# A two-layer graph network on one core: rings of eight for the last layer's rows, loaded by GpSimd, and bias rows as three bf16 parts

## The reference, cut to what matters

```python
# layer 0: messages over all edges, a sum for each destination, an MLP, two norms
m     = silu(concat(x[src], x[dst], edge_attr) @ mW1 + mb1) @ mW2 + mb2
agg   = segment_sum(m, dst, 6250)
h_new = silu(concat(x, agg) @ uW1 + ub1) @ uW2 + ub2
x1    = layernorm(x + layernorm(x + h_new) * gamma + beta)
# layer 1: the mean of the neighbours' new rows, an MLP with relu, a norm
agg   = segment_sum(x1[src], dst, 6250) / maximum(degree, 1)
h     = relu(relu(concat(x1, agg) @ W1 + b1) @ W2 + b2)
out   = layernorm(x1 + h)
```

## Time and profile before

| | |
|---|---|
| median of three runs | 2214.85 us |
| span of the profiled execution | 2215.4 us |
| TensorE busy | 1979.7 us (89%), granted clock 0.936 on average |
| VectorE busy | 1662.3 us (75%) |
| ScalarE busy | 1432.8 us (65%) |
| POOL busy | 1515.0 us (68%), with 455.7 us of "issue" between its gathers |
| DMA | 487.82 MB, mean 220 GB/s |

### The profile page before, as it was taken

How to read it: one execution, slowest core, us unless ns; L and a number is a source line. 1 busy time by engine, 2 the same in 40 slices (tenths; PEclk the granted TensorE clock), 3 DMA queues, 4 the chain that set the end, 5 groups by cost and what they waited for, 6 DMA issues and landing times.

```text
span 2215.4 us, 59812 instructions
## 1 busy us (share of the span) xinstructions
PE 1979.7 (89%) x19664; PEld 1740.5 (79%) x19664; DVE 1662.3 (75%) x5615; ACT 1432.8 (65%) x3734; POOL 1515.0 (68%) x1605
## 2 busy tenths in 40 slices
PE   7888888889988998999998999999989999999774
PEld 7877777777887887887886898987987998988542
DVE  7688877877886877887887788888887788774332
ACT  3677766776776766776776777766766766673122
POOL 7577777777777777777777777777777777770110
PEclk9999989997998997998999999999998999999976
DMA  8477767676687777777877787877877887986822
GB/s 288 139 206 219 201 189 213 175 220 202 187 231 211 210 218 210 216 239 231 241 232 210 241 249 243 269 238 219 254 244 227 272 266 238 293 264 207 268 65 62
DMA packets 307523, 487.82 MB, mean 220 GB/s; under 512 B 120202, under 2 KB 181644, under 8 KB 307208
## 3 DMA queue, kind: packets, MB, share of 16 engines
q10 hardware_dynamic: 102369, 251.46, 34.3%
q1 hardware_dynamic: 154823, 129.94, 19.8%
q0 software_dynamic: 50016, 102.53, 17.9%
HBM read 375.62 MB, written 108.13 MB: 218 GB/s over the span
## 4 chain that ended last, share of the span: by engine, by line
POOL 46%; PE 18%; issue 17%; DMA 8%; DVE 6%; ACT 2%; DVEq 1%; ACTq 0%; SPq 0%; POOLq 0%
POOL gath L858 46%; DMA gath<-P_d,src_i 6%; PE ps_l L1167 4%; PE ps_pre L1114 3%; PE ps_cnt L1131 3%; DVE edgeK L917 2%; PE ps_sum L1151 2%; DMA gath<-x1T_d 1%; DVE pre L930 1%; PE ps_pre L1225 1%; DVE edgeL L915 1%; ACT eT_c L1401 1%; PE ps_pre L1227 1%; PE ps_pre L1117 1%; PE ps_p L432 1%
## 5 line engine op out<-in xcount | busy, mean ns | idle before, releaser
L858 POOL DMA_INDIRECT gath<-P_d,src_i x1535 | 1456.8, 949 | 486.9 <-issue 455.7
L917 DVE TENSOR_SCALAR edgeK<-iotaK,key 128x500 bf16<-128x500 f16 (+1 forms) x1564 | 667.3, 488 | 0.0
L1114 PE MATMUL ps_pre<-wc,eT_c 128*128 128x128 f32 x3128 | 613.7, 318 | 2.4 <-issue 2.4
L1131 PE MATMUL ps_cnt<-edgeK,edgeL 128*128 128x250 bf16 (+1 forms) x3128 | 479.9, 301 | 92.4 <-ACT counts L1269 48.6
L1114 PEld LDWEIGHTS ps_pre<-wc,eT_c 128*128 128x128 f32 x3128 | 508.8, 204 | 25.0 <-issue 2.6
L1269 ACT ACTIVATE counts<-ps_cnt 128x1000 bf16<-128x1000 f32 x391 | 404.4, 1034 | 173.2 <-issue 85.1
L1151 PE MATMUL ps_sum<-edgeN,h 128*128 128x40 f32 x3128 | 421.8, 285 | 55.4 <-ACT h L1325 55.1
L1151 PEld LDWEIGHTS ps_sum<-edgeN,h 128*128 128x128 f32 x3128 | 391.6, 196 | 81.1 <-ACT h L1325 69.1
L930 DVE TENSOR_TENSOR pre<-ps_pre,gath 128x512 f32<-128x512 f32 x384 | 260.9, 680 | 254.9 <-DMA gath<-P_d,src_i 175.7
L1131 PEld LDWEIGHTS ps_cnt<-edgeK,edgeL 128*128 128x128 bf16 x3128 | 288.3, 101 | 162.1 <-DVE edgeK L917 83.4
L1325 ACT ACTIVATE h<-pre 128x512 f32<-128x512 f32 x391 | 243.9, 624 | 262.4 <-DVE pre L930 258.6
(11 more groups left out here) (160 smaller groups left out, 1505.5 us busy)
## 6 DMA issues: line engine op xcount, KB each, us to landing
eT_c<-eT ACTq DMA_DIRECT2D x193, 512.0 KB
A_d<-counts ACTq DMA_DIRECT2D x168, 384.0 KB
rel_c<-rel_d ACTq DMA_DIRECT2D x193, 240.0 KB
A_v<-A_d SPq DMA_DIRECT2D x70, 448.0 KB
A_v<-A_d SPq DMA_DIRECT2D x111, 256.0 KB
gath<-P_d,src_i POOLq DMA_INDIRECT x1535
A_d<-counts ACTq DMA_DIRECT2D x56, 416.0 KB
Qw<-Q_d SPq DMA_DIRECT2D x56, 180.0 KB
```

The lines of the kernel that those rows point to most:

```text
L858: pool.indirect_dma_start(gath[:, q, t * D:(t + 1) * D], None, v["P_d"], bass.IndirectOffsetOnAxis(ap=src_i[g % 2][:, c:c + 1], axis=0)).t ...
L917: last = V.tensor_scalar(edgeK[x][:, ROFF[j]:ROFF[j] + A2 * w], iotaK[j][:, :, 0:A2 * w // KR], key[k][:, q * QT + j:q * QT + j + 1], None ...
L1114: T.matmul(o, eT_c[c % RE][:, e0:e0 + P], wc[:], start=True, stop=False)
L1131: last = T.matmul(o[:, :, w0:w0 + w], edgeL[x][:, j, 0:P], r, start=(j == 0), stop=(j == QT - 1 and q == 0), skip_group_check=True)
```

## The change

Two things change. First, the rings `xT_l` and `x_l` get eight places instead of three (`RL`), in buffers that are free by then: `xT_l` takes all seven parts of `gath` and `xT_u`; `x_l` takes the second halves of the three `eT_c`, the two `h`, and `hT_u`, `z_u`, `xT1_u`. The ring of results `z_l` stays at three (`RZ`). Their loads move from ScalarE's queue to POOL's. The first eight stand ahead of POOL's first mean; the load of unit `w + 6` stands behind the mean of `w`, for `w` of 2 to 6, and waits until TensorE's step 0 and VectorE's step 3 of unit `w - 2` are done. Second, each of the three bias rows is split into three bf16 rows whose sum is the float32 row, in partitions 0, 32 and 64 of a tile of 65 partitions that is otherwise zero. TensorE multiplies 65 rows of ones with it in bf16, in one pass. VectorE makes the parts once, in six instructions for each row, at quads 14 and 21.

```diff
-    xT_l, x_l = [gath[:, i, :] for i in range(3)], [gath[:, 3 + i, :] for i in range(3)]
+    xT_l = [gath[:, i, :] for i in range(GQ)] + [xT_u]
+    x_l = [t[:, UB * D:2 * UB * D] for t in eT_c] + [t[:].rearrange("p t n -> p (t n)") for t in h] + [
+        hT_u, z_u[:].rearrange("p j n -> p (j n)"), xT1_u]
 ...
     def gpsimd(pool):
 ...
+        def load_last(w):
+            cols, n = last_columns(w)
+            r = w % RL
+            if w == 0:
+                pool.wait_ge(pre_add, NQ)
+                pool.wait_ge(sum_mm, NQ)
+            u = next(u for u, (b0, b1, s0) in enumerate(UNITS) if LAST_UNITS[w][1] <= b1)
+            if r >= 5:
+                u = len(UNITS) - 1
+            pool.wait_ge(x1_out, 16 * (u + 1))
+            pool.wait_ge(x1T_out, 16 * (u + 1))
+            if w >= RL:
+                pool.wait_ge(l_hidden, w - RL + 1)
+                pool.wait_ge(l_z, w - RL + 1)
+            pool.dma_start(xT_l[r][:, 0:n * P], v["x1T_d"][:, cols]).then_inc(l_xT_in[r], 16)
+            pool.dma_start(x_l[r].rearrange("p (j n) -> p j n", n=D)[:, 0:n, :],
+                           v["x1_d"][cols, :].rearrange("(j p) n -> p j n", p=P)).then_inc(l_x_in[r], 16)
 ...
+            for w in range(RL):
+                load_last(w)
             for w in range(len(LAST_UNITS)):
 ...
                 nc.gpsimd.tensor_tensor(sumT[:, cols], sumT[:, cols], deg[:, cols], ALU.mult).then_inc(l_mean, 1)
+                if w >= 2 and w + RL - 2 < len(LAST_UNITS):
+                    load_last(w + RL - 2)
 ...
+        def split_bias(k, whole):
+            V.tensor_copy(biases[k][0:1, :], whole[0:1, :])
+            V.tensor_copy(bias_hi[:], whole[:]).then_inc(bias_part, 1)
 ...
+            V.tensor_tensor(bias_rest[:], whole[:], bias_hi[:], ALU.subtract).then_inc(bias_part, 1)
 ...
+            V.tensor_copy(biases[k][32:33, :], bias_rest[32:33, :])
+            V.tensor_copy(bias_mid[:], bias_rest[:]).then_inc(bias_part, 1)
 ...
+            V.tensor_tensor(biases[k][64:65, :], bias_rest[64:65, :], bias_mid[64:65, :], ALU.subtract).then_inc(bias_ready, 1)
 ...
-                T.matmul(ps_y[x][:, 0:n * D], ones_row[:], b2bc[0:1, :].unsqueeze(1).broadcast_to([1, n, D]), start=True, stop=True)
+                T.matmul(ps_y[x][:, 0:n * D], onesb[0:BK, :], biases[2][:].unsqueeze(1).broadcast_to([BK, n, D]), start=True, stop=True)
 ...
-                if w + 3 < len(LAST_UNITS):
-                    load_last(w + 3)
```

More of the change, by code:

```diff
@@ L54 @@
 VB, RA, RT, LEAD, AHEAD = 14, 4, 12, 4, 10
+RL, RZ = 8, 3
 NQ = -(-(-(-N_EDGES // P)) // QT)
@@ L66 @@
 EPS = 1e-5
+BK = 65
 SKIP = 8192
@@ L245, in bass_gnn_two_layers @@
         eps_col = sb("eps_col", [P, 1])
-        ones_row = sb("ones_row", [1, P])
+        biases = [sb(f"bias{k}", [BK, D], BF16) for k in range(3)]
         rdeg_in = sem("rdeg_in")
@@ L396, in gpsimd @@
         pool.memset(onesb[:], 1.0)
-        pool.memset(v["ones_row"][:], 1.0)
+        for b in v["biases"]:
+            pool.memset(b[:], 0.0)
         pool.iota(first_i[:], [[0, 1]], base=0, channel_multiplier=GE * N_NODES // N_EDGES).then_inc(made, 1)
@@ L712, in build_edges @@
     a_in = [sem(f"av_in{r}") for r in range(RT)]
-    l_xT_in, l_x_in, l_out = ([sem(f"l_{n}{i}") for i in range(3)] for n in ("xT_in", "x_in", "out"))
+    l_xT_in, l_x_in = ([sem(f"l_{n}{i}") for i in range(RL)] for n in ("xT_in", "x_in"))
+    l_out = [sem(f"l_out{i}") for i in range(RZ)]
     l_mean, l_hidden, l_relu, l_y, l_z, l_var, l_sd, l_rs, l_norm, l_dv = (
@@ L829, in fast @@
             sp.wait_ge(dg_io, 64 * len(UNITS))
-            for r in range(3):
-                sp.wait_ge(l_out[r], 16 * len(range(r, len(LAST_UNITS), 3)))
+            for r in range(RZ):
+                sp.wait_ge(l_out[r], 16 * len(range(r, len(LAST_UNITS), RZ)))
         def general(sp):
@@ L948, in add_visit, with split_biases @@
                             ALU.add).then_inc(changed, 1)
+        def split_bias(k, whole):
+            V.tensor_copy(biases[k][0:1, :], whole[0:1, :])
+            V.tensor_copy(bias_hi[:], whole[:]).then_inc(bias_part, 1)
+            dve.wait_ge(bias_part, 3 * k + 1)
+            V.tensor_tensor(bias_rest[:], whole[:], bias_hi[:], ALU.subtract).then_inc(bias_part, 1)
+            dve.wait_ge(bias_part, 3 * k + 2)
+            V.tensor_copy(biases[k][32:33, :], bias_rest[32:33, :])
+            V.tensor_copy(bias_mid[:], bias_rest[:]).then_inc(bias_part, 1)
+            dve.wait_ge(bias_part, 3 * k + 3)
+            V.tensor_tensor(biases[k][64:65, :], bias_rest[64:65, :], bias_mid[64:65, :], ALU.subtract).then_inc(bias_ready, 1)
+        def split_biases(s):
+            if s == 2 * GQ:
+                dve.wait_ge(u_in, 160)
+                split_bias(0, ub2bc)
+                split_bias(1, bbc)
+            if s == 3 * GQ:
+                dve.wait_ge(v["l1_in"], 64)
+                split_bias(2, b2bc)
         parts = [0]
@@ L1073, in fast @@
                 unit_step(s)
+                split_biases(s)
                 if g + 1 < GROUPS and q == 2:
@@ L1187, in unit_step @@
                 pe.wait_ge(u_silu, u + 1)
-                T.matmul(ps_u[:, 0:n * D], ones_row[:], ub2bc[0:1, :].unsqueeze(1).broadcast_to([1, n, D]), start=True, stop=True)
+                if u == 0:
+                    pe.wait_ge(bias_ready, 2)
+                T.matmul(ps_u[:, 0:n * D], onesb[0:BK, :], biases[0][:].unsqueeze(1).broadcast_to([BK, n, D]), start=True, stop=True)
                 for j in range(n):
@@ L1197, in unit_step @@
                 pe.wait_ge(u_scaled, u + 1)
-                T.matmul(ps_u[:, 0:n * D], ones_row[:], bbc[0:1, :].unsqueeze(1).broadcast_to([1, n, D]), start=True, stop=True)
+                T.matmul(ps_u[:, 0:n * D], onesb[0:BK, :], biases[1][:].unsqueeze(1).broadcast_to([BK, n, D]), start=True, stop=True)
                 for j in range(n):
@@ L1223, in last_step @@
                     pe.wait_ge(l_relu, w - 1)
-                pe.wait_ge(l_xT_in[w % 3], 16 * (w // 3 + 1))
-                T.matmul(o, w1[:, 0, :], xT_l[w % 3][:, 0:n * P], start=True, stop=False)
+                pe.wait_ge(l_xT_in[w % RL], 16 * (w // RL + 1))
+                T.matmul(o, w1[:, 0, :], xT_l[w % RL][:, 0:n * P], start=True, stop=False)
                 pe.wait_ge(l_mean, w + 1)
@@ L1426, in fast @@
                 unit_step(s)
-                if s == UNITS[-1][2] + U_LEN + 1:
-                    for w in range(3):
-                        load_last(w)
                 for w, k in LAST_AT.get(s, ()):
```

38 lines of the change are left out of this document (15 added, 23 removed).

## The result

| | before | after |
|---|---|---|
| median of the runs | 2214.67 us (4 runs, 2213.88 to 2218.34) | 2163.72 us (4 runs, 2162.70 to 2164.69) |
| span of the profiled execution | 2215.4 us | 2162.5 us |

The ratio is 0.977, with a 95% interval of 0.9757 to 0.9784: 51 us less, where 43 were forecast (2172).

The account below looks back on a forecast made before the run. Gathers on POOL bound the edge loop, TensorE towards its end; after 2163 waits did. Span: 2215.4 - 47.1 (loads) + 1 (POOL) + 2 (contention) - 1 (bias) + 2 (clock) = 2172.3; median 2172 us, range 2158 to 2196.

Parts of the forecast that it names:

- The ring takes the ten waits away: Last layer: with eight places, all ten TensorE waits for the transposed rows go, 35.2 us.
- VectorE is next while visits remain: Last layer: VectorE's sums at 0.82 us set the pace; the last sum ends at 2140.8 instead of 2167.25.
- Turns of 4.1 us behind the visits: After the visits, TensorE and ScalarE alternate: 4.1 us a turn instead of 9.78, three turns, plus 2.2 us once.
- POOL's loads at 1.25 us each: Before POOL's first mean: each load costs about a 128-row gather; +1 us, range 0 to 9.
- Contention of the early loads, +2: Between 2016 and 2029, the first five pairs of loads share DMA with counts; +2 us, range 0 to 6.8.
- The clock, +2: After the visits: TensorE mostly at full clock; +2 us, range 0 to 10.
- The bias rows, -1 and 2.3 inside the turns: bf16 instead of float32: -1.0 us (-3 to 0) in layer 0, 2.3 us in the last layer's three turns.
- The same rows in layer 0: End of layer 0: gathers hide most of the bf16 saving; only units 11 and 12 count, -1.0 us (-3 to 0).
- pieces on POOL: Rival, 17%: POOL's loads priced by the piece, 5.35 us a unit, first mean 8 us late; 2178 us.
- a clock that stays at its lower level once the visits are gone: Rival, 12%: TensorE's clock stays at its lower level after the visits; 2180 us.
- waits that turn into others: Rival, 8%: visits wait for counts or a free bank instead, losing half the gain up to the last sum; 2190 us.
- POOL held up by VectorE: Rival, 3%: VectorE slows POOL's descriptor writing, eight units' loads cost 113 us, first mean 70 us late; 2238 us.

Follow-up runs that it names:

- e5: The changed kernel with rings of four instead of eight and the loads on ScalarE behind the norm; 2165.45 us, ratio 0.9773 to the kernel before.
- e6: The changed kernel with rings of three, loads on ScalarE behind the root (step 4) instead of the norm; 2164.12 us, ratio 0.9768 to before.
- e9: The changed kernel with the last layer's bias row as the float32 row of ones again; 2170.85 us, ratio 0.9807 to before.
- e10: The changed kernel with all eight first loads waiting for the last unit's stores; 2163.20 us, ratio 0.9777 to before.
- e3: The changed kernel with rings of eight kept, but all loads on ScalarE behind the norm; 2167.72 us, ratio 0.9783 to before.
- e8: The changed kernel with VectorE reading all base registers of a place ahead of its first sum; 2175.65 us, ratio 0.9822 to before.
- e2: The changed kernel's new loads alone, with the float32 bias rows of before; 2175.17 us, ratio 0.9819 to before.
- e4: The changed kernel with rings of three instead of eight, loads still on POOL; 2164.44 us, ratio 0.9774 to before.
- e7: The changed kernel with each load cut into four, so POOL issues eight a unit instead of two; 2163.81 us, ratio 0.9766 to before.
- e1: The kernel before with only the bf16 bias rows, rings of three still loaded by ScalarE; 2208.52 us, ratio 0.9974 to before.

## Why the prediction was right, step by step

- **The ring takes the ten waits away.** Right; and the reason that the prediction gives (the load stands behind the norm) is what e5 and e6 show. The norm in the turn of the earlier trace rows is that of two units before, not of the unit before, and it is late because the relu of w + 2 stands ahead of it. The prediction didn't say that depth and queue are of no account.
- **VectorE is next while visits remain.** Right: sums 0.82 us apart, last one's end forecast at 2140.8, found at 2135.88. The 4.9 us are the head start, and not a faster pace: from 2088.6 on, where the forecast counts 46 sums and six steps 3, before has 45 sums left (the one at 2087.98 had ended) and six steps 3, and after has 42 and five. The three sums and the step 3 are 4.5 us, the sum counted too many 0.8. Of this, the loop's last sum over edges came 2.6 us earlier and the first mean 3.3. TensorE's 14.0 us of waits for a free bank say the same, and e9 most of all: nine products longer by some 0.8 us each moved the last sum by 1.1.
- **Turns of 4.1 us behind the visits.** 3.78 in after. The hold of 2.2 us (a relu behind a norm and a store) is found once, at the first turn: products end at about 2133.9, relu at 2136.81. The last store's issue came at 2155.01, forecast 2160.2; from the last sum's end that is 19.1 us, forecast 19.4.
- **POOL's loads at 1.25 us each.** Wrong in size by half: 0.57 and 0.80, 1.3 us a pair. Of no effect, as the first mean still waits for VectorE (4.65 us idle). 512 pieces cost 0.23 us more than 128. The Trainium skill, "DMA: Bandwidth & Descriptors", section on the anatomy of one DMA on the gpsimd path, says that many descriptors can be emitted before their incremental cost shows. The trace agrees in the main: 384 pieces more show as those 0.23 us.
- **Contention of the early loads, +2.** Between 0 and 0.4 us (e10).
- **The clock, +2.** In after's profile nothing: 1.00 over the three turns, and 0.75 from 2136 on, against 0.64 before. In e3 to e8 and e10, with the same turns, the first one took 5.3 to 6.5 us instead of 3.78. So 1.5 to 2.7 us are the usual price, which is what the forecast put, and that this profile shows none of it is luck.
- **The bias rows, -1 and 2.3 inside the turns.** The term that was mis-sized: 3.3 us forecast for both parts, 10.8 found (e2 against after). The product itself takes 0.22 us (2110.04 to 2110.26 in the timeline), near the 0.3 of the estimate, and 0.39 on the chain behind a wait. In the last layer the thirteen products gave 7.2 us in the profiles of e9 and after, and not 2.3: 1.1 before the last sum, 2.2 directly and 3.9 beside them, by the clock. From the last sum's end to the span's end e9 takes 32.6 us and after 26.6, but e4 to e7 and e10 take 28.0 to 30.7. Against those the last layer's share is 3.1 to 5.7 us. The rows' own length accounts for 3.3 us (1.1 and 2.2); that the rest is theirs isn't shown.
- **The same rows in layer 0.** The forecast was 1 us (0 to 3). The last sum over edges starts at 2015.33 and 2016.58 in the two kernels with float32 rows in layer 0 and between 2008.45 and 2013.91 in the eleven with bf16 rows, at 2010.89 in the middle one. By these profiles, one of each, some 5 us come from there. e1 agrees, with 5.8 us (2.9 to 8.6) where the last layer could gain little; e2 against e9 gives 0.12%, 2.7 us, within overlapping intervals. Between 2000 and 2018 TensorE is busy for 17.9 to 18.0 us in all thirteen kernels, so what it owes at the last gather is paid in full there. How many of layer 0's products count, between the four that I let count and all 26, the runs don't settle.
- **The sum.** 43 us forecast, 51 found: loads 40 (e2), bias rows 11 on top. The forecast erred by 8.3 us, 7.5 of them on the side of the bias rows. That the loads' 40 us meet the 39.8 of the forecast is in part luck: in e2 the last sum ends 2.8 us before the forecast's place for it, and the rest takes 1.6 us longer, with one turn at 7.79 us where the next has 4.71. In after's own profile the span is 9.8 us under the forecast's 2172.3: 4.9 to the last sum, 0.3 behind it, 0.6 behind the last store, and the 4 us that the forecast adds for POOL, contention, bias and clock and that this profile doesn't show beside them.

The rivals: pieces on POOL, refuted by 0.80 and e7; a clock that stays at its lower level once the visits are gone, refuted as a state (three turns at 1.00), though one turn usually has it; waits that turn into others, only the 14.0 us for a bank (5.3 before); POOL held up by VectorE, refuted by 0.57 for a load; faster sums, not faster, but the sums began earlier. None of the variants is measurably faster than after.

## What to carry to other kernels

A ring that looks too short can be one whose refill is issued too late, as here: look at what stands between the last reader and the issue before adding places. A saving on an engine that isn't the bound is worth what the alternating stages without cover hold of it, so count those turns, and give the clock a term there. Before pricing such a turn from one profile, look at the same turn in the profiles of the variants: here it was 3.78 us in one kernel and 5.3 to 6.5 in seven others. Where an engine reads a register between two dependent instructions, part of the read may be hidden there; count it before moving it.

## What the hardware showed that I had not expected

- A plain load issued by POOL costs it 0.57 us for 128 rows of 2 KB, 0.80 for 512 pieces of 512 bytes, and 0.57 for a quarter of either. From issue to landing the transposed rows took 5.5 us in after (median of 11), 3.4 in e4 from 2050 on (of 9) through the same queue of POOL's, and 3.3 before (of 12) through ScalarE's. So the queue alone doesn't make after's longer. Its first five, issued up to 2020 and in flight while DMA's share rose to 0.99, took 6.4 us, its last four 5.1; what else they wait for isn't shown.
- A register read costs VectorE 0.34 us between two dependent sums and 0.58 us in a row of four.
- TensorE behind a wait can run a whole turn at its lower level with no more idle than in a kernel that kept the full clock: 3.65 us ahead of it in e7 (clock 0.56) and in after (1.00); e10's 1.53 and 1.72 us for step 0 stand where after has 0.86 and 0.87. What decides it stays open.
- A bf16 bias product takes 0.22 us in a row of work and 0.39 us when it is the first behind a wait; the float32 one 1.05 and 1.12. So the first product behind a wait pays, beside its length, 0.07 to 0.17 us.
